# Storing a mixture-of-experts output before the last expert's rows are in, and adding those rows in memory by one accumulating transfer

## The chip, the cores and the metric

The kernel runs on one core of a Trainium2 chip. The metric is device time in microseconds (us) of one execution. The kernel before the change was timed three times: 296.11 us in the median, with 294.85 as the lowest and 299.49 as the highest.

## What is computed

One transformer block on an input `x` of 2 x 1024 tokens of 128 floats: a layer norm with a modulation, a gated DeltaNet attention with 16 heads of 8, a residual, a second layer norm, and then a mixture of experts. The last part is what the change is about:

```python
probs = softmax(h @ router_w.T)                     # 8 experts
k_probs, k_idx = top_k(probs, 2); k_probs /= sum    # two experts per token
# each expert takes its first `capacity` = 641 pairs (token, choice); later pairs give 0
h1 = silu(buf @ w1); out_buf = h1 @ w2              # per expert: 641x128 -> 512 -> 128
pair_out = out_buf[flat_e, slot] * keep
combined = sum over the token's two pairs of pair_out * k_probs
x = x + gb * (combined + h)
```

All is float32. There are 2048 tokens, 4096 pairs, and the output is 2048 x 128 floats, 1.05 MB.

## The kernel before, in words

Each engine has its own written program; the order of the work on an engine is the order of its code, and semaphores join the engines. The 2048 tokens are cut into four groups of 512 (`GROUPS = 4`), a group into four tiles of 128 tokens (`TG = 4`).

Attention, norms and routing run group by group up to about 192 us. In that time the rows that go to the experts are written by indirect transfers of GpSimd (POOL) into a table `dispatched` in memory. The residual with the gated normalised input stays in the on-chip tile `X`.

Then the eight experts follow, two buffers in turn (`u` is 0 or 1, `i` counts pairs of experts). For each one SyncE (SP) loads 640 rows and the weights, TensorE (PE) multiplies up (line 1876) and down (line 1893), ScalarE (ACT) applies silu (line 948), VectorE (DVE) scales the rows by the routing weight and the gate (line 1407), and POOL scatters them, 128 rows at a time, into the memory table `pair_out` (line 685). The 641st row of every expert is handled apart and scattered by line 698, seven experts' rows in a first transfer and the last expert's in a second.

`pair_out` has two parts, both cleared to zero early in the program. Rows 0 to 4095 hold one row per pair, for the first seven experts. Rows 4096 to 6143, 1.05 MB, are a table with one row per token, for the last expert alone; a token picks an expert at most once, so each token has at most one row there. The constant `to_token` turns a pair's row number into its token's row number for that.

The end of the program, after the scatters of the first seven experts have landed, goes so:

- SP loads the pair part in four transfers of 512 KB (line 599) into `yb`.
- DVE, per group, adds the two pairs of each token (`pair_sums`, line 1462) and the residual (`with_input`, line 1467) into `ys`. Between the first two of these it scales the very last 128 rows of the last expert.
- SP and ACT wait until the last expert's scatters have all landed (semaphores `rows_out1` and `last_rows_out`, lines 600, 601, 950 and 951), and then load the token part in four transfers of 256 KB into `yt` (line 603 by SP for groups 0 and 2, line 952 by ACT for groups 1 and 3).
- DVE adds `yt` to `ys` into `yo` (line 1478), group by group.
- SP and ACT store `yo` to the output (lines 606 and 955), 256 KB a group, and SP waits for the four stores (line 607).

Of the kernel before, what the change touches and what calls it, by code (L numbers as in the profile page):

```python
# [8 lines left out]
ALU = mybir.AluOpType  # L9
# [4 lines left out]
P = 128  # L14
B, S, DM = 2, 1024, 128
# [3 lines left out]
NE, FF = 8, 512  # L19
TOPK = 2  # L20
NTOK = B * S
PAIRS = NTOK * TOPK
# [6 lines left out]
TG = 4  # L29
GPB = S // (TG * P)  # L30
GROUPS = B * GPB
# [39 lines left out]
COL, _at = {}, 0  # L71
# [8 lines left out]
def constants():  # L80

    c = np.zeros((P, NCONST), np.float32)
    p = np.arange(P)
    r, t = p[:, None], p[None, :]
    same = r // BLK == t // BLK
    c[:, COL["ident"]] = np.eye(P)
    for i in range(NSUB):
        ref = (t // BLK) * BLK + i * SUB
        plus = same & (r >= ref) & (r <= t)
        minus = same & (r < ref) & (r > t)  # L90
        c[:, COL["gk"]][:, i * P:(i + 1) * P] = plus.astype(np.float32) - minus
        c[:, COL["kbias"]][:, i] = np.where(p % BLK < (i + 1) * SUB, 0.0, -1e4)
        c[:, COL["qbias"]][:, i] = np.where((p % BLK) // SUB == i, 0.0, -1e4)
    c[:, COL["own"]] = (r // SUB == t // SUB) & (r <= t)
    c[:, COL["cq"]] = same & (r <= t)
    c[:, COL["ck"]] = same & (r > t)
    c[:, COL["later"]] = np.where(r % BLK > t % BLK, -2.0 ** 100, 0.0)
    c[:, COL["hmask"]] = (p // DH % HG)[:, None] == np.arange(HG)[None, :]
    c[:, COL["smask"]] = (p // (C * DH))[:, None] == (np.arange(SW) // E1)[None, :]
    c[:, COL["tri"]] = r < t  # L100

    c[:, COL["spread"]] = r % (HALF * C) == t // DH
    col = np.arange(TG * 2 * BPT)[None, :] // BPT
    c[:, COL["tile_half"]] = (p // (HALF * C))[:, None] == col
    c[:, COL["blk"]] = (p // BLK)[:, None] == np.arange(BPT)[None, :]
    inv = (1.0 / 10000.0 ** (np.arange(0, DH, 2, dtype=np.float32) / np.float32(DH))).astype(np.float32)
    ang = (np.arange(S, dtype=np.float32)[:, None] * inv[None, :]).astype(np.float32)
    tab = lambda f: np.tile(f(ang).astype(np.float32).reshape(S // P, P, ROPE_HALF).transpose(1, 0, 2).reshape(P, -1), (1, B))
    c[:, COL["cos"]] = tab(np.cos)
    c[:, COL["sin"]] = tab(np.sin)  # L110

    c[:, COL["keep"]] = (np.arange(GROUPS) % GPB != 0)[None, :]
    c[:, COL["iota"]] = np.arange(NE)[None, :]
    g, at = np.divmod(np.arange(GROUPS * TG * TOPK), TG * TOPK)
    c[:, COL["pid"]] = (g * P + r) * TG * TOPK + at
    c[:, COL["to_token"]] = PAIRS + (g * P + r) * TG + at // TOPK - c[:, COL["pid"]]
    c[:, COL["batch_at"]] = np.where(p == NE - 1, PAIRS + NTOK // B, PAIRS // B)[:, None]
    c[:, COL["skip_last"]] = np.where((p == NE - 1)[:, None] == np.array([True, False])[None, :], 1e6, 0.0)
    return c
# [3 lines left out]
SYNC_OUT = list(range(0, GROUPS, 2))  # L123
SCALAR_OUT = list(range(1, GROUPS, 2))
# [30 lines left out]
def program(nc, x_d, wall_d, wo_d, rows_d, rwt_d, w1_d, w2_d, ct_d, wmod_d, const_d, bo_d, out_d):  # L155
    x_v = x_d.rearrange("b (g t p) c -> (b g) p t c", t=TG, p=P)
    out_v = out_d.rearrange("b (g t p) c -> (b g) p t c", t=TG, p=P)
    disp_d = nc.dram_tensor("dispatched", [ROWS, RW], F32, kind="Internal").ap()
    pair_d = nc.dram_tensor("pair_out", [PAIRS + NTOK, DM], F32, kind="Internal").ap()
    pair_v = pair_d[0:PAIRS, :].rearrange("(g p n) c -> g p (n c)", g=GROUPS, p=P)  # L160
    token_v = pair_d[PAIRS:PAIRS + NTOK, :].rearrange("(g p n) c -> g p (n c)", g=GROUPS, p=P)

    def w1_v(e):
        return w1_d[bass.ds(e, 1), :, :].rearrange("e p f -> p (e f)")
# [5 lines left out]
    with ctx:  # L170
# [3 lines left out]
        def sem(name):  # L174
            return ctx.enter_context(nc.semaphore(name))
# [3 lines left out]
        def event(name, per, ahead=None):  # L179
            e = Event(sem(name), per, ahead)  # L180
            if ahead:
                ahead_of[ahead].append(e)
            return e
# [36 lines left out]
        def carver():  # L220
            at = [0]

            def carve(*shape):
                n = int(np.prod(shape))
                v = arena[:, at[0]:at[0] + n]
                at[0] += n
                assert at[0] <= ARENA
                names = "abcd"[:len(shape)]
                return v.rearrange(f"p ({' '.join(names)}) -> p {' '.join(names)}", **dict(zip(names, shape)))

            return carve

        carve = carver()
# [69 lines left out]
        carve = carver()  # L303
# [12 lines left out]
        orow = carve(2, CT, DM)  # L316
        yb = carve(GROUPS, TG, TOPK, DM)
        ys = carve(GROUPS, TG, DM)
        yo = carve(GROUPS, TG, DM)
        yt = carve(GROUPS, TG, DM)  # L320
        row_gate = carve(CT, DM)
        gate_d = carve(DM)
        last_gate = carve(DM)
# [135 lines left out]
        osc = [event(f"rows_out{u}", 16 * CT) for u in range(2)]  # L459
        outs_left = [event(f"outs_left{u}", 1, "sp") for u in range(2)]  # L460
        s_lastO, s_lastR, s_lastS = sem("last_out_T"), sem("last_out_rows"), sem("last_rows_out")

        s_yb = [sem(f"pairs_in{g}") for g in range(GROUPS)]
        s_yt = [sem(f"tokens_in{g}") for g in range(GROUPS)]
        gates_done = event("row_gates", CT + 2)
        s_prep = sem("last_rows_prepared")

        s_ys, s_yo = sem("pairs_combined"), sem("out_ready")
        s_out = sem("out_written")

        def made(n, a):
# [31 lines left out]
        def rows_made(e, a):  # L503

            return a + 1 + (a > last_at(e))
# [7 lines left out]
        def apart(eng):  # L513


            eng.sem_inc(s_apart, 1)
# [7 lines left out]
        def _(sp):  # L524
# [72 lines left out]
            sp.wait_ge(osc[0].sem, osc[0].now(NE // 2 - 1) + 16)  # L597
            for g in range(GROUPS):
                sp.dma_start(yb[:, g].rearrange("p t k c -> p (t k c)"), pair_v[g]).then_inc(s_yb[g], 16)
            sp.wait_ge(osc[1].sem, osc[1].now(NE // 2 - 1))  # L600
            sp.wait_ge(s_lastS, 16)
            for g in SYNC_OUT:
                sp.dma_start(yt[:, g].rearrange("p t c -> p (t c)"), token_v[g]).then_inc(s_yt[g], 16)
            for g in SYNC_OUT:
                sp.wait_ge(s_yo, g + 1)
                sp.dma_start(out_v[g], yo[:, g]).then_inc(s_out, 16)
            sp.wait_ge(s_out, 16 * GROUPS)


        @block.gpsimd  # L610
        def _(pool):
# [68 lines left out]
            def rows_out(u, i, lo, hi):  # L680

                for a in range(lo, hi):
                    pool.wait_ge(r_done[u].sem, r_done[u].now(i, rows_made(2 * i + u, a)))
                    apart(pool)
                    pool.indirect_dma_start(pair_d, bass.IndirectOffsetOnAxis(ap=meta[:, u, a, 0:1].bitcast(U32), axis=0),  # L685
                                            orow[:, u, a, :], None, bounds_check=PAIRS + NTOK - 1, oob_is_err=False).then_inc(osc[u].sem, 16)
# [6 lines left out]
            def last_rows_out(n):  # L693

                pool.wait_ge(s_prep, 3)
                pool.wait_ge(s_lastR, n + 1)
                apart(pool)
                pool.indirect_dma_start(pair_d, bass.IndirectOffsetOnAxis(ap=last_idx[:, n:n + 1], axis=0),  # L698
                                        lastR[:, n, :], None, bounds_check=PAIRS + NTOK - 1, oob_is_err=False).then_inc(osc[0].sem if n == 0 else s_lastS, 16)
# [2 lines left out]
            rows_out(1, NE // 2 - 1, 0, FA)  # L702
            last_rows_out(1)
            rows_out(1, NE // 2 - 1, FA, CT)


        @block.scalar
        def _(act):
# [231 lines left out]
            for i in range(NE // 2):  # L940
                for u in range(2):
                    for k, (f, n) in enumerate(UPS):
# [3 lines left out]
                            act.wait_ge(r_ps[u].sem, r_ps[u].before(i))  # L946
                            act.wait_ge(last_done[u].sem, last_done[u].before(i))
                        a_.activation(hid[:, u, f, c0:c0 + cn], ps[:, k % 4, 0:cn], ACT.Silu).then_inc(hid_done[u].sem, 1)  # L948
            act.wait_ge(osc[1].sem, osc[1].now(NE // 2 - 1))
            act.wait_ge(s_lastS, 16)  # L950
            for g in SCALAR_OUT:
                act.dma_start(yt[:, g].rearrange("p t c -> p (t c)"), token_v[g]).then_inc(s_yt[g], 16)
            for g in SCALAR_OUT:
                act.wait_ge(s_yo, g + 1)
                act.dma_start(out_v[g], yo[:, g]).then_inc(s_out, 16)


        @block.vector
        def _(dve):
            v_ = nc.vector  # L960
# [4 lines left out]
            for u in range(2):  # L965
                f = v_.memset(v1[:, u, :, :, DH:E1], 1.0)
# [497 lines left out]
            def with_input(g):  # L1464

                dve.wait_ge(s_ys, 2 * g + 1)
                v_.tensor_tensor(ys[:, g].rearrange("p t c -> p (t c)"), ys[:, g].rearrange("p t c -> p (t c)"), X[:, g], ALU.add).then_inc(s_ys, 1)
# [4 lines left out]
            for g in range(1, GROUPS):  # L1472
                pair_sums(g)
                with_input(g)
            for g in range(GROUPS):
                dve.wait_ge(s_ys, 2 * g + 2)
                dve.wait_ge(s_yt[g], 16)
                v_.tensor_tensor(yo[:, g], ys[:, g], yt[:, g], ALU.add).then_inc(s_yo, 1)  # L1478


        @block.tensor
# [478 lines left out]
```

## Time and profile before

| what | us |
|---|---|
| median of three runs (lowest, highest) | 296.11 (294.85, 299.49) |
| the profiled execution | 293.68 |
| its span, first to last instruction | 291.9 |
| last matrix product ends | about 276.7 |
| last `ys` of the four groups ready | 281.98 |
| last scatter of the last expert landed | 281.95 |
| last `yo` ready | 287.88 |

The time of an execution is 1.8 us longer than its span. Over the span PE is busy for 86%, DVE for 72%, ACT for 42% and POOL for 31%; these are averages over stages, and in the last 15 us PE does nothing. An engine's name with a q (SPq, ACTq, POOLq) stands for its queue, where transfers are issued. A transfer has two times: that of its issue and the time to landing, counted from the start of the issue to the moment at which its semaphore is complete.

### The profile page before, as it was taken

What the parts mean: (1) busy time and instruction counts of PE and PEld (TensorE: products, weight loads), DVE (VectorE), ACT (ScalarE), POOL (GpSimd) and SP (SyncE); (2) the same over time, 40 slices, a digit from 0 to 9 for tenths busy, and PEclk for the clock granted to TensorE, in tenths of its full rate; (3) what the DMA queues carried; (4) which work ended last, traced back from release to release, by engine and by line L of the source; (5) the groups of instructions that cost most, each with busy time, mean ns of one, the idle gap of its engine ahead of it and who ended that gap; (6) DMA issues with size and microseconds to landing.
All of it is one profiled execution on the core that took longest, in us unless ns stands there. A gap on an engine that the chain in (4) does not pass through costs nothing. (4 is left out here: it accounts for less than half of the span.)

```text
span 291.9 us, 11345 instructions
## 1 busy us (share of the span) xinstructions
PE 251.4 (86%) x4731; PEld 188.4 (65%) x4731; DVE 209.2 (72%) x828; ACT 121.2 (42%) x274; POOL 90.0 (31%) x102
## 2 busy tenths in 40 slices
PE   7997898799977999899887889988999999999900
PEld 3665657676566855678555564436898889888800
DVE  5697989849699597986778568837557655756563
ACT  4598258652668444753322122203233432343200
POOL 0030014000023406052134216740544464546630
PEclk9999579779998799955999596999999999999965
DMA  6980000030700103000021001122424433331566
GB/s 178 338 311 4 3 2 6 4 146 4 291 4 4 30 3 112 13 4 12 22 80 46 21 6 57 45 80 86 129 55 130 147 96 108 121 100 36 172 214 227
DMA packets 18197, 25.19 MB, mean 86 GB/s; under 512 B 2679, under 2 KB 11400, under 8 KB 18146
## 3 DMA queue, kind: packets, MB, share of 16 engines
q1 hardware_dynamic: 14434, 19.18, 20.5%
q0 software_dynamic: 2368, 4.24, 4.5%
q10 hardware_dynamic: 1344, 1.05, 1.1%
q8 instruction: 37, 0.61, 0.9%
q14 instruction: 14, 0.11, 0.1%
HBM read 12.84 MB, written 12.15 MB: 86 GB/s over the span
## 5 line engine op out<-in xcount | busy, mean ns | idle before, releaser
L948 ACT ACTIVATE arena<-ps 128x385 f32<-128x385 f32 (+1 forms) x64 | 27.6, 439 | 62.3 <-PE ps L1876 61.6
L685 POOL DMA_INDIRECT pair_out<-arena,meta x40 | 39.2, 981 | 45.0 <-DVE arena L1407 19.2
L631 POOL DMA_INDIRECT dispatched<-row,idx x32 | 32.5, 1014 | 60.2 <-PE ps L1619 27.6
L1893 PE MATMUL ps<-w2t,arena 128*128 128x128 f32 x320 | 40.4, 278 | 0.0
L1893 PEld LDWEIGHTS ps<-w2t,arena 128*128 128x128 f32 x320 | 39.3, 191 | 0.9
L1512 PE MATMUL ps<-later_b,ident_b 128*128 128x512 bf16 x141 | 38.1, 409 | 0.0
L1876 PE MATMUL ps<-arena,w1t 128*128 128x256 f32 (+1 forms) x128 | 37.6, 434 | 0.2 <-issue 0.2
L1407 DVE SCALAR_TENSOR_TENSOR arena<-ps,meta,arena 128x128 f32<-128x128 f32 x40 | 14.0, 351 | 26.4 <-PE ps L1893 15.4
L654 POOL TENSOR_TENSOR arena<-arena,ex 128x256 f32<-128x256 f32 x16 | 10.7, 695 | 68.2 <-DVE arena L1029 50.2
L1612 PE MATMUL ps<-v,wts 32*32 32x9 f32 x2048 | 24.0, 180 | 8.8 <-issue 6.5
L1612 PEld LDWEIGHTS ps<-v,wts 32*32 32x32 f32 x2048 | 22.0, 117 | 13.5 <-issue 13.1
L1876 PEld LDWEIGHTS ps<-arena,w1t 128*128 128x128 f32 x128 | 22.9, 190 | 10.1 <-issue 0.9
L1507 PE MATMUL ps<-const,arena 128*128 128x128 f32 x120 | 21.1, 316 | 4.8 <-DVE arena L1029 3.0
L1512 PEld LDWEIGHTS ps<-later_b,ident_b 128*128 128x128 bf16 x141 | 13.6, 104 | 14.2 <-issue 3.9
L1507 PEld LDWEIGHTS ps<-const,arena 128*128 128x128 f32 x120 | 16.7, 165 | 8.1 <-DVE arena L1029 3.4
L1072 DVE SCALAR_TENSOR_TENSOR arena<-arena,dec,ps 128x18 f32<-128x18 f32 x128 | 19.7, 230 | 0.0
L827 ACT COPY s_sb<-ps 128x512 f32<-128x512 f32 x16 | 9.2, 577 | 23.0 <-PE ps L1654 23.0
L1541 PE MATMUL ps<-wall,hT 128*128 128x384 f32 x32 | 14.8, 590 | 0.7 <-ACT arena L753 0.5
L1654 PE MATMUL ps<-arena,fkT 32*32 32x128 f32 x512 | 13.2, 295 | 0.0
L978 DVE BATCH_NORM_STATS2 st<-ps 128x6 f32<-128x128 f32 x16 | 3.7, 287 | 13.2 <-PE ps L1694 13.2
L1009 DVE TENSOR_TENSOR arena<-arena,const 128x256 f32<-128x256 f32 x32 | 11.4, 420 | 2.1 <-ACT arena L753 2.0
L1094 DVE SCALAR_TENSOR_TENSOR wts<-s_sb,ps 128x512 f32<-128x512 f32 x16 | 10.9, 683 | 1.6 <-ACT s_sb L827 1.6
(182 smaller groups left out, 446.3 us busy)
## 6 DMA issues: line engine op xcount, KB each, us to landing
dispatched<-fill SPq DMA_DIRECT2D x12, 260.0 KB, 4.2
pair_out<-zero SPq DMA_DIRECT2D x6, 512.0 KB, 3.4
arena<-dispatched SPq DMA_DIRECT2D x8, 325.0 KB, 3.0
w1t<-in_w SPq DMA_DIRECT2D x8, 256.0 KB, 2.7
w2t<-in_w SPq DMA_DIRECT2D x8, 256.0 KB, 3.1
arena<-pair_out SPq DMA_DIRECT2D x4, 512.0 KB, 5.1
const<-in_constants SPq DMA_DIRECT2D x1, 803.5 KB, 6.5
X<-in_x SPq DMA_DIRECT2D x1, 768.0 KB, 7.6
```

Source lines behind the costliest of these rows:

```text
L631: pool.indirect_dma_start(disp_d, bass.IndirectOffsetOnAxis(ap=idx[:, p.g, t, k:k + 1], axis=0), row[:, p.g, t, k, :], None, bounds_check= ...
L685: pool.indirect_dma_start(pair_d, bass.IndirectOffsetOnAxis(ap=meta[:, u, a, 0:1].bitcast(U32), axis=0), orow[:, u, a, :], None, bounds_ch ...
L948: a_.activation(hid[:, u, f, c0:c0 + cn], ps[:, k % 4, 0:cn], ACT.Silu).then_inc(hid_done[u].sem, 1)
L1072: v_.scalar_tensor_tensor(state[:, (n + 1) % NB, a, :], state[:, n, a, :], dec[:, g % 2, at:at + 1], U_ps[:, a, j, :], ALU.mult, ALU.add). ...
L1407: v_.scalar_tensor_tensor(orow[:, u, a, :], row_bank(u, a)[:, 0:P], meta[:, u, a, 1:2], row_gate[:, a, :], ALU.mult, ALU.mult).then_inc(r_ ...
L1507: return nc.tensor.transpose(out, in_, ident[0:in_.shape[0], 0:in_.shape[0]])
L1512: mm(bank.rearrange("p (n c) -> p n c", c=P), ident_b[:], later_b[:].unsqueeze(1).to_broadcast([P, 4, P]), start=True, stop=True)
L1541: mm(proj_bank(g, t)[:, 0:3 * DM], hT[:, t * P:(t + 1) * P], wall[:, 0:3 * DM], start=True, stop=True).then_inc(proj.sem, 1)
L1612: mm(O_ps[r, h * E1:(h + 1) * E1], wts[r, t % 2, h, :], v1[r, g % 2, t, h, :], start=(h == 0), stop=False, skip_group_check=True, tile_pos ...
L1654: f = mm(ps[j * BLK:(j + 1) * BLK, hg, at:at + P], st(r), mv_(r), skip_group_check=True, tile_position=(hg * 32, j * BLK), **kw)
L1876: mm(ps[:, k % 4, 0:cn], w1t[:, u, f * P:(f + 1) * P], bT[:, u, c0:c0 + cn], start=True, stop=True).then_inc(up_ps[u].sem, 1)
L1893: m = mm(row_bank(u, a)[:, 0:P], hid[:, u, f, 1 + a * P:1 + (a + 1) * P], w2t[:, u, f, :], start=(f == 0), stop=(f == FT - 1))
```

## The change

The token part of `pair_out` is no longer loaded, and `yt` and `yo` are gone. SP and ACT store `ys`, the sum without the last expert's rows, as soon as DVE has it for a group. When the four stores and the last expert's scatters have all landed, POOL issues one transfer from memory to memory that adds the 1.05 MB token part to the output (`accum_op=ALU.add`). For this the token part is laid out in the order of the tokens, as the output is, which changes the constant `to_token`. SP waits for that transfer at the end.

```diff
-    c[:, COL["to_token"]] = PAIRS + (g * P + r) * TG + at // TOPK - c[:, COL["pid"]]
+    c[:, COL["to_token"]] = PAIRS + (g * TG + at // TOPK) * P + r - c[:, COL["pid"]]
...
-    token_v = pair_d[PAIRS:PAIRS + NTOK, :].rearrange("(g p n) c -> g p (n c)", g=GROUPS, p=P)
+    token_rows = pair_d[PAIRS:PAIRS + NTOK, :].rearrange("(r n) c -> r (n c)", r=P)
+    out_rows = out_d.rearrange("b s c -> (b s) c").rearrange("(r n) c -> r (n c)", r=P)
...
             for g in range(GROUPS):
                 sp.dma_start(yb[:, g].rearrange("p t k c -> p (t k c)"), pair_v[g]).then_inc(s_yb[g], 16)
-            sp.wait_ge(osc[1].sem, osc[1].now(NE // 2 - 1))
-            sp.wait_ge(s_lastS, 16)
             for g in SYNC_OUT:
-                sp.dma_start(yt[:, g].rearrange("p t c -> p (t c)"), token_v[g]).then_inc(s_yt[g], 16)
-            for g in SYNC_OUT:
-                sp.wait_ge(s_yo, g + 1)
-                sp.dma_start(out_v[g], yo[:, g]).then_inc(s_out, 16)
+                sp.wait_ge(s_ys, 2 * g + 2)
+                sp.dma_start(out_v[g], ys[:, g]).then_inc(s_out, 16)
             sp.wait_ge(s_out, 16 * GROUPS)
+            sp.wait_ge(s_added, 16)
...
             rows_out(1, NE // 2 - 1, FA, CT)
+            pool.wait_ge(osc[1].sem, osc[1].now(NE // 2 - 1))
+            pool.wait_ge(s_lastS, 16)
+            pool.wait_ge(s_out, 16 * GROUPS)
+            pool.dma_start(out_rows, token_rows, accum_op=ALU.add, max_dma_last_dim=4096).then_inc(s_added, 16)
...
-            act.wait_ge(osc[1].sem, osc[1].now(NE // 2 - 1))
-            act.wait_ge(s_lastS, 16)
             for g in SCALAR_OUT:
-                act.dma_start(yt[:, g].rearrange("p t c -> p (t c)"), token_v[g]).then_inc(s_yt[g], 16)
-            for g in SCALAR_OUT:
-                act.wait_ge(s_yo, g + 1)
-                act.dma_start(out_v[g], yo[:, g]).then_inc(s_out, 16)
+                act.wait_ge(s_ys, 2 * g + 2)
+                act.dma_start(out_v[g], ys[:, g]).then_inc(s_out, 16)
...
-            for g in range(GROUPS):
-                dve.wait_ge(s_ys, 2 * g + 2)
-                dve.wait_ge(s_yt[g], 16)
-                v_.tensor_tensor(yo[:, g], ys[:, g], yt[:, g], ALU.add).then_inc(s_yo, 1)
```

Nothing ahead of these places moves on any engine. The end of POOL's program (`rows_out1` is landings of the last scatters, `out_written` landings of the stores), before and then now:

```order
L698 DMA pair_out<-lastR,last_idx 6144x128 [waits last_rows_prepared,last_out_rows]
L685 DMA pair_out<-arena,meta 6144x128 [waits rows_done1] x2
L170 UNCONDITIONAL_BRANCH
```

```order
L694 DMA pair_out<-lastR,last_idx 6144x128 [waits last_rows_prepared,last_out_rows]
L681 DMA pair_out<-arena,meta 6144x128 [waits rows_done1] x2
L704 DMA out<-pair_out 256x1024 [waits out_written,last_rows_out,rows_out1]
L171 UNCONDITIONAL_BRANCH
```

POOL has one transfer more, of 256 pieces of 1024 floats (4 KB), behind all its scatters and behind the four stores. The end of ACT's program, before and then now (`pairs_combined` is the count of DVE's steps on `ys`, `out_ready` that of `yo`):

```order
L948 ACTIVATE arena<-ps 128x256 [waits up_ps1] x4
L952 DMA arena<-pair_out 128x512 [waits last_rows_out,rows_out1]
L952 DMA arena<-pair_out 128x512
L955 DMA out<-arena 128x4x128 [waits out_ready] x2
L170 UNCONDITIONAL_BRANCH
```

```order
L948 ACTIVATE arena<-ps 128x256 [waits up_ps1] x4
L951 DMA out<-arena 128x4x128 [waits pairs_combined] x2
L171 UNCONDITIONAL_BRANCH
```

ACT's two loads are gone, and its stores now wait for `ys`, no longer for `yo`; SP's end changes in the same way.

## Rows read from the trace of the kernel before

**Rows 1.** Chain of waits, its end: start us, us, what.

```profile
277.95 1.44 POOLq L170
279.39 0.30 issue
279.70 2.25 DMA pair_out<-arena,meta
281.95 0.02 issue
281.97 3.32 DMA arena<-pair_out
285.28 0.03 issue
285.31 0.02 DVEq L1477
285.33 0.04 issue
285.38 0.20 DVE arena L1478
...
286.92 0.09 issue
287.00 0.87 DVEq L170
```

**Rows 2.** Timeline, the last 12 us: start us, us, engine, line, op.

```profile
279.90 0.69 DVE L1467 TENSOR_TENSOR arena<-arena,X 128x512 f32<-128x512 f32 x1
280.56 0.69 DVE L1462 TENSOR_TENSOR arena<-arena 128x512 f32<-128x512 f32 x1
281.29 0.69 DVE L1467 TENSOR_TENSOR arena<-arena,X 128x512 f32<-128x512 f32 x1
...
285.38 2.50 DVE L1478 TENSOR_TENSOR arena<-arena 128x512 f32<-128x512 f32 x4 [3.40 <-DMA arena<-pair_out]
...
286.70 1.66 ACTq L955 DMA_DIRECT2D out<-arena  x2
```

**Rows 3.** ACT's stores, line 955: duration ns, starts, then time to landing.

```profile
L955 ACTq DMA_DIRECT2D out<-arena x2: 457/780/1102, 286.7 to 287.9; - x2
...
DMA to landing us min/median/max: 3.4/3.5/3.5
```

**Rows 4.** SP's stores, line 606, the same view.

```profile
L606 SPq DMA_DIRECT2D out<-arena x2: 388/388/389, 286.1 to 287.3; - x2
...
DMA to landing us min/median/max: 2.6/3.0/3.3
```

**Rows 5.** SP's four loads of the pair part, line 599, the same view.

```profile
L599 SPq DMA_DIRECT2D arena<-pair_out x4: 326/426/433, 272.7 to 274.0; - x4
...
DMA to landing us min/median/max: 3.6/5.1/6.5
```

**Rows 6.** ACT's two loads of the token part, line 952, the same view.

```profile
L952 ACTq DMA_DIRECT2D arena<-pair_out x2: 361/406/450, 282.0 to 282.4; - x2
...
DMA to landing us min/median/max: 3.6/4.0/4.5
```

**Rows 7.** Busy time of engines by stretch; last two columns: DMA share, GB/s.

```profile
273.70:280.10 6.40, 2.97 (x22) 2.56 (x20) 4.47 (x11) 1.16 (x3) 4.88 (x6) 0.97 0.97 352
283.20:286.00 2.80, 0.00 (x0) 0.00 (x0) 0.62 (x2) 0.00 (x0) 0.00 (x0) 0.50 0.97 360
287.00:291.00 4.00, 0.00 (x0) 0.00 (x0) 0.88 (x2) 0.00 (x0) 0.00 (x0) 0.50 0.85 262
...
280.00:281.00 1.00, 0.00 (x0) 0.00 (x0) 1.00 (x2) 0.00 (x0) 0.71 (x1) 0.50 0.10 26
281.00:282.00 1.00, 0.00 (x0) 0.00 (x0) 0.94 (x2) 0.00 (x0) 0.00 (x0) 0.50 0.14 41
```

**Rows 8.** Timeline, POOL's last three scatters (the first of eight rows).

```profile
276.57 1.24 POOL L698 DMA_INDIRECT pair_out<-lastR,last_idx  x1 [0.30 <-DVE arena L1407]
...
278.11 1.28 POOL L685 DMA_INDIRECT pair_out<-arena,meta  x1 [0.30 <-issue]
...
279.70 1.02 POOL L685 DMA_INDIRECT pair_out<-arena,meta  x1 [0.30 <-issue]
```

More of the change, by code:

```diff
@@ L318, in program @@
         ys = carve(GROUPS, TG, DM)
-        yo = carve(GROUPS, TG, DM)
-        yt = carve(GROUPS, TG, DM)
         row_gate = carve(CT, DM)
@@ L463, in program @@
         s_yb = [sem(f"pairs_in{g}") for g in range(GROUPS)]
-        s_yt = [sem(f"tokens_in{g}") for g in range(GROUPS)]
+        s_added = sem("last_expert_added")
         gates_done = event("row_gates", CT + 2)
         s_prep = sem("last_rows_prepared")
-        s_ys, s_yo = sem("pairs_combined"), sem("out_ready")
+        s_ys = sem("pairs_combined")
         s_out = sem("out_written")
```

## The prediction

> **What bounds the kernel now.** I read the chain of waits first, from its end backwards. It says that after the last matrix product only transfers and short adds are left [rows 1]: POOL's last scatter starts at 279.70 and has landed 2.25 us later, at 281.95; the load of the token part starts at 281.97 and the first group of it is there 3.32 us later; DVE adds, and the last part is the stores. The reader should see that 281.95 is a double point. DVE's last add of the residual starts at 281.29 and takes 0.69 us, so the last `ys` is ready at 281.98, 0.03 us after the scatter has landed [rows 1, 2]. Both branches of the tail, "sums without the last expert" and "rows of the last expert in memory", are ready at one time. All before that is the same in both kernels, so the prediction is about the 9.9 us from 281.98 to the span's end at 291.9.
>
> Those 9.9 us split so: token loads until DVE's first add at 285.38, which is 3.4 us; the four adds with their small gaps until 287.88, 2.5 us [rows 2]; ACT's last store, issued at 287.9 and landed 3.5 us later at 291.4 [rows 3]; and 0.5 us from there to the end. These are three steps in a row: read, add, write.
>
> The transfers are next, since the change trades one kind for another. A transfer here has a part that doesn't depend on its size. The four pair loads carry 4 x 512 KB = 2.10 MB: the first is issued at 272.7, the last at 274.0 and that one lands 6.5 us later, at 280.5; 7.8 us in all [rows 5]. The four token loads carry 1.05 MB: first issue 281.97 [rows 1], the last issue at 282.4, landed 4.5 us later at 286.9; 4.9 us in all [rows 6]. The difference is 2.9 us for 1.05 MB, so T = 2.0 us + 2.9 us for every 1.05 MB. The rates agree with that: 352 GB/s over the middle of the pair loads and 360 over that of the token loads, with the DMA engines 97% busy in both [rows 7]. Stores, which go in pieces of 512 bytes, run at 262 GB/s [rows 7]. POOL's last scatter, 64 KB, needs 2.25 us from its start to landing [rows 1], so a transfer issued by POOL has a fixed part of about 2.25 - 0.2 = 2.05 us, the same as above.
>
> **The change part by part.**
>
> *Taken away.* The four token loads and the wait for them (3.4 us), DVE's four adds (2.5 us). After 281.98 the old tail had load, add, store, end: 3.4 + 2.5 + 3.5 + 0.5 = 9.9 us, and only the last two kinds of term stay.
>
> *Stores of `ys`.* Groups 0, 1 and 2 are ready at about 278, 279.3 and 280.6 and their stores are out of the way early. The last isn't: its store can start only at 281.98. In the old tail the last stores took 3.3 and 3.5 us with two or three others in flight, and the first one, alone, 2.6 us [rows 3, 4]. Group 2's store, issued 1.4 us ahead, is still moving, so I take 3.3 us; ends 2.6 and 3.5.
>
> *What the early stores collide with.* From 277.9 to 280.5 the DMA engines are full of the pair loads [rows 7], and DVE has no slack: it begins the last pair sum at 280.56, just when the last load has landed (280.5) [rows 2, 5]. Group 0's store stands on SP's own queue behind the pair loads. Group 1's goes by ACT's queue, beside the last load. Its 0.26 MB is worth 0.26/0.36 = 0.7 us of transfer time if all of it went first, and less than half of the time does it overlap. I take 0.3 us on the last `ys`; ends 0 and 0.7. POOL's last scatter may be delayed too, which costs nothing: it is now needed only when the last store has landed, 3.6 us later.
>
> *The new wait.* POOL waits for scatters and stores; nothing is queued behind the transfer on POOL, and only SP's end waits for it. The scatters have long landed by then, so it is the store that holds it. From the release to the start of POOL's instruction I take 0.3 us, the gap that stands before each of its scatters [rows 8].
>
> *The accumulating transfer.* The trace of before has no such transfer, and none from memory to memory. Bounds from rows: it must at least move 1.05 MB, and if only that counts it costs what the token loads cost, 4.9 us. If all three passes (read the table, read the output, write it) count, at the rate of the stores, it is 2.05 + 3.15/0.262 = 14.1 us. Between them lies the case in which the two reads set the pace and the write runs beside them: 2.10 MB of reads in pieces of 4 KB is just what the pair loads are, 7.8 us. I take that, since in size, piece and direction of its reads that row is nearest; POOL's handling of 256 pieces in place of 128 I leave in it, because a scatter of 8 rows takes POOL 1.24 us and one of 128 rows 1.02 to 1.28 [rows 8]: it isn't the number of rows that costs.
>
> Here a page speaks for a smaller number. By the Trainium skill, "DMA: Bandwidth & Descriptors", section "Anatomy of one DMA — SWDGE (gpsimd) path", a transfer issued by GpSimd takes 2.0 us plus its bytes at 436 GB/s, 4.4 us for 1.05 MB, and the sum would be 3.4 us less than mine. The loads here ran at 352 and 360 GB/s, so the trace doesn't bear out the rate, though it does the 2.0 us. Another page speaks against the change: "Collectives: The Full Stack", section "The bandwidth ceiling: the fold count and why AG ≠ RS ≠ AR", says that a reducing transfer reads two sources through one read queue and so moves its result at half the rate of a copy, not that the add itself costs. No run here has shown that yet; it would put the transfer where the pair loads' row does.
>
> *The end.* 0.5 us from the last landing to the span's end, as before.
>
> *DVE, ACT, SP elsewhere.* The constant's change moves the last expert's rows in memory and leaves their number and size alone; nothing earlier in any engine's order changes. Costed at nothing; the cover for the scatters is the 3.6 us named above.
>
> **The sum.** 281.98 + 0.3 + 3.3 + 0.3 + 7.8 + 0.5 = 294.2 us of span, against 291.9: 2.3 us more. The old tail of 9.9 us becomes one of 12.2. The profiled execution took 293.68 us, so a like one would take 296.0. It lies 2.4 us under the median of the three runs (296.11), which scatter over 4.6 us. I set the difference on the median: 296.11 + 2.3 = 298.4 us.
>
> In short: two transfers follow each other in both tails. The change takes away an add of 2.5 us and starts the first of the two no earlier, and its second transfer carries two or three times the bytes of the store it replaces.
>
> **The rivals.** The price of the accumulating transfer decides, so the cases are cut by it. Each 2% is 5.9 us, which is also about what three runs that scatter by 4.6 us can tell from no change.
>
> *Forecast, 0.60.* The transfer takes 5.9 to 11.4 us, and the total is 296.5 to 302.0, most likely 298.4.
>
> *Rival 1, it is slow, 0.24.* Place: the memory-to-memory transfer. Mechanism: each piece needs its two reads and the write one behind the other, so that three passes are paid, not two. At 14.1 us it gives 298.4 + 6.3 = 304.7 us. It decides from 11.4 us on (7.8 + 5.9 - 2.3). For it: no row shows reads and writes of memory overlapped in one transfer, and the stores ran at 262 GB/s. Against it: the stores' pieces were 512 bytes and these are 4 KB.
>
> *Rival 2, the adding is nearly free, 0.14.* The second read hides and the transfer costs what a copy does, 4.9 us, and the last store, with nearly no company, lands in 2.6 us with no collision: 281.98 + 2.6 + 0.3 + 4.9 + 0.5 = 290.3, or 1.6 us less than before: 294.5 us. For it: the fixed part is the same for POOL. Against it: the DMA engines were at 97% with one read stream at 360 GB/s, so there's no room for a second. (The figure that the Trainium skill's "DMA: Bandwidth & Descriptors" gives, above, would come out on this side.)
>
> *Rival 3, the early stores take back time, within the above.* If all 0.79 MB of them stood before the last pair load and the last store, at 262 GB/s that is 3.0 us in place of the 0.3 I charged: 301.1 us. For it: the loads fill the engines until 280.5. Against it: from 280.5 to 281.98 the DMA engines are 10 to 14% busy, at 26 and 41 GB/s [rows 7], and the early stores can use that. I give it a tenth of the forecast's chance.
>
> *It doesn't do what it says, 0.02.* The stores would start early only for three groups out of four; that is in the sum. What is left is a gain that I don't see.
>
> Faster by over 2% would need a total of 290.2, under every case here: 0.02. Slower by over 2% is rival 1: 0.24. Within 2%: 0.74. The range has to hold 8 in 10: 295.3 leaves out the cheapest half of rival 2, and 304.5 the worst part of rival 1.
>
> **What would show it.** In the new profile: DVE's last add still ends at 282.0 to 282.6; the last store on ACT's queue starts right then and takes 2.6 to 3.5 us; POOL starts its transfer at 285.4 to 286.0, and its landing is 7.8 us later; in the DMA row the rate of bytes read from memory in that stretch is twice that of bytes written to it, near 350 GB/s for the reads. What would make the prediction wrong: a transfer that takes clearly more or less than 7.8 us from POOL's start; a DVE that waits for the last pair load by more than 0.7 us; or a POOL that needs several us before the first byte moves, which no row here shows.

## The result, and the profile after

The changed kernel takes 300.31 us in the median of four runs (299.07 to 303.9), the kernel before 295.48 us (its three runs of 296.11 in the median, and one more). The ratio is 1.0177, 95% interval [1.0108, 1.0247]: 3.2 to 7.3 us more, 5.2 us at the ratio itself. The interval takes in 2%, so whether the change costs more or less than 2% is not shown. Forecast were 2.3 us more. The total lies in the range and the sign is right; the size isn't, and the missing 2.9 us are the subject of what follows.

The ratios and intervals, here and below, leave out the slow runs, those over 1.5% above the kernel's fastest, and the profiled execution of the changed kernel is one of these (303.9 us). It is already 5 us late when the pair loads begin (277.7 us, against 272.7 before). Nothing in the code ahead of that place was changed, and in twelve profiles of ten kernels that stretch begins anywhere from 272.6 to 278.8 us. The two groups hardly overlap, though: it begins at 272.6 to 274.6 us in the four profiles of kernels with the old order of the token part, and at 274.4 to 278.8 in the eight with the new one, in whole or in part. Whether that is the change or chance is not shown. To compare what the change was meant to do, I measure the tail, from SP's first pair load to the end of the span. It was 291.9 - 272.7 = 19.2 us and 19.4 in the second profile of the kernel before; it is 302.1 - 277.7 = 24.4 us and 24.5 in the second profile of the changed one. The difference is 5.2 us, the same as that of the timed runs. A second timing of both doesn't narrow it: one execution of the changed kernel took 298.95 us and three took 305, and eleven of the kernel before took from 294.54 to 304.57.

The end of the chain of waits of the changed kernel (start us, us, what), which answers to [rows 1]:

```profile
286.72 0.70 DVE arena L1463
287.43 0.02 issue
287.45 2.48 DMA out<-arena
289.93 0.03 issue
289.95 0.04 POOLq L703
290.00 0.56 issue
290.56 1.04 POOLq L171
```

The last `ys` is ready at 287.43, ACT's last store lands 2.48 us later at 289.93, and POOL starts its transfer at 290.58. The chain stops there; what comes next has to be looked up by line. Line 704, POOL's accumulating transfer, and then line 171, where the closing instructions of all engines stand (engine, op, count: duration in ns, start):

```profile
L704 POOL DMA_DIRECT2D out<-pair_out x1: 1020/1020/1020, 290.6 to 290.6; - x1
...
DMA to landing us min/median/max: 8.1/8.1/8.1
```

```profile
L171 POOLq DRAIN  x1: 11284/11284/11284, 290.6 to 290.6; - x1
L171 SPq COMPARE_BRANCH  x1: 33/33/33, 298.8 to 298.8; - x1
L171 SPq DRAIN  x1: 74/74/74, 299.3 to 299.3; - x1
L171 SPq EVENT_SEMAPHORE  x1: 17/17/17, 302.0 to 302.0; - x1
L171 ACTq EVENT_SEMAPHORE  x1: 17/17/17, 302.0 to 302.0; - x1
```

The transfer lands at 298.7, 8.1 us after its start, and SP goes on at 298.8. But POOL's DRAIN, the closing instruction on its queue, runs from 290.56 for 11.28 us: until 301.84, which is 3.1 us after the landing. The last step of every engine, SP's and ACT's among them, starts only at 302.0, though ACT's own drain was over at 288.1: the engines meet at the end, and POOL is the last to come. In the list of waits of SP's queue the same 3 us look so:

```profile
SPq L603 <- DMA out<-pair_out: 12.5, 1, 12.5
...
SPq L171 <- PEq L171: 2.7, 1, 2.7
```

The second row names PE. PE had been done since 282, so the name is wrong; the row's use is that it says 2.7 us, where the kernel before has 0.2. Read the drains then.

The kernel before has this drain too, and its trace shows it:

```profile
L170 POOLq DRAIN  x1: 8888/8888/8888, 278.0 to 278.0; - x1
```

It ran from 277.95 to 286.84, 4.9 us past the landing of the last scatter at 281.95, and nobody waited for it, because loads, adds and stores went on until 291.4. In the second profile of the kernel before it ended 5.2 us ahead of the end of the span.

The accumulating transfer itself in the stretches view (last columns: DMA share and GB/s):

```profile
293.00:297.00 4.00, 0.00 (x0) 0.00 (x0) 0.00 (x0) 0.00 (x0) 0.00 (x0) 0.50 1.03 199
```

The DMA engines are as busy as in [rows 7], and the rate counted is only 199 GB/s. Behind the landing they have next to nothing to do: from 299 to 300 us their share is 0.02, and from 300 to 302 it is 0.00, while POOL's drain goes on.

### The profile page after: what moved, and what is told of

Same layout as the page of the kernel before. It is cut to its first block and busy times, and to the rows that moved or that the text cites. A ratio compares the mean times of both kernels' runs of the same rounds, so it can differ in the third digit from the quotient of the medians.

```text
span 302.1 us, 11334 instructions
## 1 busy us (share of the span) xinstructions
PE 253.1 (84%) x4731; PEld 189.3 (63%) x4731; DVE 206.6 (68%) x824; ACT 121.3 (40%) x274; POOL 92.0 (30%) x103
## 3 DMA queue, kind: packets, MB, share of 16 engines
HBM read 12.84 MB, written 13.20 MB: 86 GB/s over the span
## 5 line engine op out<-in xcount | busy, mean ns | idle before, releaser
L627 POOL DMA_INDIRECT dispatched<-row,idx x32 | 33.6, 1051 | 62.2 <-PE ps L1611 28.5
L1504 PE MATMUL ps<-later_b,ident_b 128*128 128x512 bf16 x141 | 35.6, 388 | 0.0
L1403 DVE SCALAR_TENSOR_TENSOR arena<-ps,meta,arena 128x128 f32<-128x128 f32 x40 | 14.0, 351 | 26.5 <-PE ps L1885 14.1
L1868 PEld LDWEIGHTS ps<-arena,w1t 128*128 128x128 f32 x128 | 22.9, 190 | 10.1 <-issue 0.9
L1604 PE MATMUL ps<-v,wts 32*32 32x9 f32 x2048 | 22.6, 177 | 6.5 <-issue 4.6
L1604 PEld LDWEIGHTS ps<-v,wts 32*32 32x32 f32 x2048 | 20.7, 111 | 10.8 <-issue 10.4
L1499 PE MATMUL ps<-const,arena 128*128 128x128 f32 x120 | 21.8, 321 | 6.0 <-DVE arena L1025 3.3
L974 DVE BATCH_NORM_STATS2 st<-ps 128x6 f32<-128x128 f32 x16 | 3.7, 285 | 14.2 <-PE ps L1686 9.9
```

What stands on the lines that cost most here:

```text
L627: pool.indirect_dma_start(disp_d, bass.IndirectOffsetOnAxis(ap=idx[:, p.g, t, k:k + 1], axis=0), row[:, p.g, t, k, :], None, bounds_check= ...
L1403: v_.scalar_tensor_tensor(orow[:, u, a, :], row_bank(u, a)[:, 0:P], meta[:, u, a, 1:2], row_gate[:, a, :], ALU.mult, ALU.mult).then_inc(r_ ...
L1499: return nc.tensor.transpose(out, in_, ident[0:in_.shape[0], 0:in_.shape[0]])
L1504: mm(bank.rearrange("p (n c) -> p n c", c=P), ident_b[:], later_b[:].unsqueeze(1).to_broadcast([P, 4, P]), start=True, stop=True)
L1604: mm(O_ps[r, h * E1:(h + 1) * E1], wts[r, t % 2, h, :], v1[r, g % 2, t, h, :], start=(h == 0), stop=False, skip_group_check=True, tile_pos ...
L1868: mm(ps[:, k % 4, 0:cn], w1t[:, u, f * P:(f + 1) * P], bT[:, u, c0:c0 + cn], start=True, stop=True).then_inc(up_ps[u].sem, 1)
```

## The experiments

All times "in the tail" count from the first pair load.

**POOL stores the last group, in the kernel before.** Is it this transfer, or any by POOL at the end, that leaves the drain exposed?

```diff
+            pool.wait_ge(s_yo, GROUPS)
+            pool.dma_start(out_v[GROUPS - 1], yo[:, GROUPS - 1]).then_inc(s_outp, 16)
...
-            for g in SCALAR_OUT:
+            for g in SCALAR_OUT[:-1]:
```

> The kernel before, with one edit: the store of the last group of the output is issued by POOL in place of ACT. In the changed kernel 3.1 us lie between the landing of POOL's transfer and the end of POOL's drain, the closing instruction of its program. Theory A (any transfer by POOL at the end leaves its drain exposed, whatever it carries): POOL's drain ends about 3 us after this store has landed, and the total is 2.5 to 4.5 us over the kernel before (3 us of drain, 0.6 us of slower issue by POOL). Theory B (only a long or accumulating transfer has that wait): the drain ends within 0.5 us of the landing and the total is 0 to 1.2 us over the kernel before.

Ratio to the kernel before 1.0189 [1.0082, 1.0296]; tail 23.0 us, 3.8 more. Its line 708 and POOL's drain:

```profile
L708 POOL DMA_DIRECT2D out<-arena x1: 810/810/810, 288.4 to 288.4; - x1
...
DMA to landing us min/median/max: 3.5/3.5/3.5
```

```profile
L170 POOLq DRAIN  x1: 7039/7039/7039, 288.3 to 288.3; - x1
```

The store starts at 288.38 and lands at 291.86, after the same 3.5 us as ACT's [rows 3]; it starts 0.5 us later in the tail than ACT's did. The drain ends at 288.35 + 7.04 = 295.39, 3.5 us after that. A plain store of 256 KB by POOL has the same wait behind it: theory A. In the old kernel, the choice of the engine that issues the last store is worth 3.8 us of tail.

**The copy without adding, by POOL.** The token part is copied over the output, which leaves all other sums out.

```diff
-            pool.dma_start(out_rows, token_rows, accum_op=ALU.add, max_dma_last_dim=4096).then_inc(s_added, 16)
+            pool.dma_start(out_rows, token_rows, max_dma_last_dim=4096).then_inc(s_added, 16)
```

> The changed kernel without the adding: POOL's last transfer copies the 1.05 MB token part over the output, which leaves the other sums out of the result. Theory A (the second read sets the accumulating transfer's pace): data moves at 350 GB/s or more, the transfer lands 4.9 to 5.5 us after POOL's start in place of 8.1, and the total is 2.6 to 3.2 us under the changed kernel. Theory B (memory to memory is slow by itself, or POOL's pieces are): 7.5 to 8.1 us, total the same. Either way POOL's drain ends about 3 us after the landing.

Ratio to the kernel before 1.0034 [0.9964, 1.0104]. Its transfer, and the DMA engines while it moves:

```profile
L704 POOL DMA_DIRECT2D out<-pair_out x1: 632/632/632, 287.2 to 287.2; - x1
...
DMA to landing us min/median/max: 5.2/5.2/5.2
```

```profile
289.00:291.50 2.50, 0.00 (x0) 0.00 (x0) 0.00 (x0) 0.00 (x0) 0.00 (x0) 0.50 0.91 365
```

5.2 us in place of 8.1, tail 21.4 in place of 24.4, and the drain ends 3.1 us after the landing again. The copy moves at 365 GB/s and the adding transfer at 199, with busy engines in both. So adding costs 2.9 us here, and that much of theory A is shown; its reason, a second read, is not. The page's count of bytes is the same for the changed kernel and for the copy:

```profile
HBM read 12.84 MB, written 13.20 MB: 86 GB/s over the span
```

This is the line of the changed kernel. The kernel before has 12.84 MB read too, and 12.15 written. So no second read of 1.05 MB is counted: either this count leaves it out, or the 2.9 us are some other cost of adding that grows with the bytes. The first fits the price, since a second read of 1.05 MB costs 2.9 us by [rows 5, 6]. The Trainium skill, "Collectives: The Full Stack", section "The bandwidth ceiling: the fold count and why AG ≠ RS ≠ AR", says of collective operations that a reduction moves at half the rate of a copy because it reads two sources. The trace agrees with the rate, at 0.55 of the copy's, and can't show the reason.

**The copy without adding, by SP.**

```diff
             sp.wait_ge(s_out, 16 * GROUPS)
+            sp.dma_start(out_rows, token_rows, max_dma_last_dim=4096).then_inc(s_added, 16)
             sp.wait_ge(s_added, 16)
```

> The same copy without adding, issued by SP in place of POOL, after the same waits. Theory A (POOL's part costs its drain, 3 us, and about 0.5 us of issue): against the copy by POOL the total is 3 to 4 us less, and the span ends 0.3 to 0.7 us after the landing. Theory B (the 3 us stand behind any memory-to-memory transfer): the same 3 us after the landing here, total 0 to 1 us under the copy by POOL.

Only the profile is telling: the medians are 297.77 us and 297.87 for the kernel before, without an interval. The transfer:

```profile
L605 SPq DMA_DIRECT2D out<-pair_out x1: 618/618/618, 289.0 to 289.0; - x1
...
DMA to landing us min/median/max: 5.4/5.4/5.4
```

```profile
L171 POOLq DRAIN  x1: 8868/8868/8868, 282.4 to 282.4; - x1
L171 SPq COMPARE_BRANCH  x1: 38/38/38, 294.4 to 294.4; - x1
...
L171 SPq EVENT_SEMAPHORE  x1: 17/17/17, 294.7 to 294.7; - x1
```

It lands as the other copy does, 5.4 us after its start, and the span ends 0.4 us later: POOL's drain, now behind its last scatter again, was over at 291.24. The tail is 17.8 us, 3.6 less than with the same copy by POOL. So the 3 us belong to the issuing engine and not to transfers from memory to memory: theory A. The timed runs don't show these 3.6 us: the medians of the two copies, 298.57 us by POOL and 297.77 by SP, are 0.8 us apart, with runs that scatter by over 6.

**Adding by group.** Four accumulating transfers, each behind its own group's store.

```diff
-            pool.wait_ge(s_out, 16 * GROUPS)
-            pool.dma_start(out_rows, token_rows, accum_op=ALU.add, max_dma_last_dim=4096).then_inc(s_added, 16)
+            for g in range(GROUPS):
+                pool.wait_ge(s_outg[g], 16)
+                pool.dma_start(out_rows[g], token_rows[g], accum_op=ALU.add, max_dma_last_dim=4096).then_inc(s_added[g], 16)
```

> The changed kernel with its one accumulating transfer cut into four, one per group, each waiting only for its own group's store. Theory A (the time goes into a serial chain of last store, then 1.05 MB accumulated, then drain): only the last 0.26 MB stand behind the last store; the last transfer lands 3.5 to 4.5 us after its start in place of 8.1, total 3.5 to 4.5 us under the changed kernel, 0.5 to 1.5 us over the kernel before. Theory B (the accumulating transfers run one after the other with a cost each, 2 us or more of it fixed): the last one queues behind the three ahead of it and lands 6 us or more after its start, total within 2 us of the changed kernel.

Ratio to the kernel before 1.0226 [1.0061, 1.0391]; tail 22.7 us. Line 706:

```profile
L706 POOL DMA_DIRECT2D out<-pair_out x4: 917/1234/1417, 286.7 to 288.8; - x4
...
DMA to landing us min/median/max: 4.4/5.9/7.0
```

The last one needs 7.0 us for a quarter of the bytes, since it stands behind the others; from the first start to the last landing it is 9.0 us (286.7 to 295.8). Cutting wins 1.7 us of tail against the one transfer, not 3.5 to 4.5: theory B. The first of the four starts 2.7 us earlier in the tail than the one transfer, but all four together take 0.9 us longer. The timed runs don't show a gain (1.0226 against 1.0177, with wide intervals). The drain ends 3.2 us after the last landing.

**Pieces of 8 KB** in the accumulating transfer (`max_dma_last_dim=8192`).

> The changed kernel with pieces of 8 KB in place of 4 KB in the accumulating transfer, 128 in place of 256. Theory A (bytes read set its pace): 8.1 us again, within 0.3 us. Theory B (a cost for each piece, in POOL or in the DMA engines): 1 us or more less.

```profile
L704 POOL DMA_DIRECT2D out<-pair_out x1: 956/956/956, 288.7 to 288.7; - x1
...
DMA to landing us min/median/max: 7.8/7.8/7.8
```

Half as many pieces and 0.3 us at most: the number of pieces isn't the price. That is what theory A expected, but it only rules out a cost for each piece; it doesn't show what the bytes wait for. One execution of this kernel was timed (301.71 us).

**Stores held back** until all four sums are ready.

```diff
-                sp.wait_ge(s_ys, 2 * g + 2)
+                sp.wait_ge(s_ys, 2 * GROUPS)
```

(and the same on ACT)

> The changed kernel, but no group's sums are stored before all four are ready. Theory A (the early stores delay the last pair load, and with it the last sum, by about 0.4 us, and win 1.5 to 2.5 us by being out of the way): last sum ready 9.3 us after the first pair load's issue in place of 9.7, but the last store lands 4.0 to 5.0 us after that in place of 2.5; the span's end comes 1.2 to 2.2 us later than in the changed kernel, 25.6 to 26.6 us after the first pair load. Theory B (early stores win nothing, since the stores are limited elsewhere): the end within 0.5 us of the changed kernel's.

The last sum is ready at 9.4 us in the tail, the last store landed at 14.9, 5.5 us later, and the tail is 27.1 us, 2.7 more than the changed kernel's. So the early stores are worth 2.7 us, more than the 1.2 to 2.2 I had expected. This is one profile; its execution, the only one timed, took 307.01 us. What they cost can't be told: the last `ys` is ready at 9.7 and 10.1 us in the two profiles of the changed kernel and at 9.3 with pieces of 8 KB, but at 9.3 and 9.7 in the two of the kernel before, which has no early stores.

**The changed kernel and the kernel before, once more.**

> The changed kernel once more, unedited, for a second profile. If the split read from its first profile holds, then from the first pair load's issue to the span's end it takes 24.4 us again (19.2 in the kernel before): accumulating transfer 8.1 us, and 3.1 us from its landing to the end of POOL's drain. If the first profile was a disturbed one, the stretch is shorter by 1 us or more.

> The kernel before once more, unedited, for a second profile. The stretch from the first pair load's issue to the span's end repeats within 0.2 us of 19.2, and POOL's drain ends 4 to 5 us after its last scatter has landed, about 4.8 us before the end of the span, so that nobody waits for it. What differs from profile to profile is the time at which that stretch begins.

Changed: tail 24.5 us, transfer 7.9, drain's end 3.1 us after its landing. Before: tail 19.4 us, drain's end 14.2 in the tail, 5.2 before the end. The splits hold.

**Half added, half the old way.** Groups 0 and 1 stored early and then added in memory by one transfer of 0.52 MB, groups 2 and 3 as before.

```diff
+    own = np.where(g < ADDED, (g * TG + at // TOPK) * P + r, (g * P + r) * TG + at // TOPK)
...
+            pool.wait_ge(s_early, 16 * ADDED)
+            pool.dma_start(out_rows, token_rows, accum_op=ALU.add, max_dma_last_dim=4096).then_inc(s_added, 16)
...
-            for g in range(GROUPS):
+            for g in range(ADDED, GROUPS):
                 dve.wait_ge(s_ys, 2 * g + 2)
                 dve.wait_ge(s_yt[g], 16)
```

> A mixture: groups 0 and 1 are stored early and get the last expert's rows by one accumulating transfer of 0.52 MB; groups 2 and 3 go the old way, load, add, store. If it is POOL's drain and the serial chain that cost the change its time, both branches run beside each other here: POOL's transfer starts about 10.3 us after the first pair load's issue, lands 5 to 6 us later, its drain ends 3.2 us after that, at 18.5 to 19.5 us; the old branch ends at 17.5 to 18.5. Total against the kernel before: 0 to 0.7 us less. If the two branches slow each other in the DMA engines by more than their overlap wins: 0.5 to 2 us more than before.

```profile
L176 POOLq DRAIN  x1: 8727/8727/8727, 286.7 to 286.7; - x1
...
L176 SPq COMPARE_BRANCH  x1: 37/37/37, 294.0 to 294.0; - x1
```

The tail is 19.2 us, no shorter than before. SP has both branches at 294.0, and POOL's drain ends at 286.65 + 8.73 = 295.38: without it the tail would be near 18, by estimate (294.0 - 276.4 and the 0.4 us of the end). The two branches do run beside each other; the drain takes the win back. The timed runs say more, though: a ratio of 1.019 [1.0113, 1.0268]. The tail doesn't show these 1.9%, so they lie ahead of it: the profiled execution begins its tail at 276.4 us, against 272.7 and 274.6 in the two of the kernel before. Ahead of the tail this kernel's instructions are those of the kernel before; only the rows of the token part are in another order, as in the changed kernel. Why it starts late is open, and with it whether the new order costs time there.

**The old tail in eight pieces**, each half a group, nothing by POOL.

```diff
-                sp.dma_start(out_v[g], yo[:, g]).then_inc(s_out, 16)
+            q.dma_start(out_v[g][:, t0:t0 + 2], yo[:, g, t0:t0 + 2]).then_inc(s_out, 16)
```

(loads and adds cut in the same way)

> The kernel before with its last three steps (load the token part, add, store) cut into eight pieces of half a group in place of four of one group; no POOL transfer at the end. If the old tail is a chain in which the stores, at 262 GB/s, begin only when the first load of 256 KB has landed and been added, a first piece half as large lands 0.5 to 0.8 us earlier and the add is 0.35 us shorter: from the first pair load's issue to the span's end 17.9 to 18.6 us in place of 19.2, a total 0.2 to 0.4% less than before, which the timed runs can hardly show. If the cost of issuing twice as many transfers (0.4 us each on SP and ACT) stands on the path instead, 19.2 us or more.

Ratio 0.9973 [0.9943, 1.0003]; tail 19.0 us. A miss, between the two: the first store starts 0.8 us earlier than before (12.6 against 13.4 in the tail), but the last one 0.9 us later (16.1 against 15.2). The last load is issued 1.7 us after the first, in place of 0.4, and lands 1.3 us later in the tail (15.5 against 14.2); DVE waits 1.0 us for the fifth half, and a half's add takes 0.42 us, not 0.35. How much of that is the issuing of more transfers, and how much the first stores moving beside the last loads, isn't told apart. Faster by 0.3% if at all, and not shown beyond the noise.

## Why the prediction was right in sign and short in size

The steps of the sum, with the times of the changed kernel's first profile (second one in brackets):

| step | forecast | measured |
|---|---|---|
| last `ys` ready, later than before | 0.3 | 0.4 (0.8) |
| last store to landing | 3.3 | 2.5 (2.5) |
| release to POOL's start | 0.3 | 0.65 (0.65) |
| accumulating transfer | 7.8 | 8.1 (7.9) |
| last landing to the end of the span | 0.5 | 3.3 (3.3) |
| tail against before | +2.3 | +5.2 (+5.3) |

- **The double point** held: what the change takes away and what it adds both begin at the last `ys`.
- **The accumulating transfer** is right in size: 7.8 forecast, 8.1 and 7.9 measured. The choice of the pair loads [rows 5] as the nearest row is borne out in its price: the copy costs 5.2 us, nearly the lower bound of 4.9, and adding costs what a second read of 1.05 MB would. That it is a second read stays argued. The sign that I had named for it, a rate of reads near 350 GB/s and twice that of writes, wasn't seen: the view gives 199 GB/s, and the bytes counted are those of a copy. Rival 1 (14.1 us) and rival 2 (4.9 us) are out by the time measured.
- **The last store** was charged 0.8 us too much: the early stores leave the DMA engines nearly to it alone, and it takes what the first store took in [rows 4]. The collision that I charged 0.3 us for isn't seen apart from the spread between profiles. Rival 3 is out: holding the stores back costs 2.7 us.
- **The gap at POOL** is 0.65 us, not 0.3: the 0.3 us of [rows 8] are the time behind POOL's own instruction before, while here 0.56 us of "issue" stand behind the end of the queue's wait, in both profiles of the changed kernel.
- **The end** is the step that failed. "0.5 us from the last landing to the span's end, as before", and with it "nothing is queued behind the transfer on POOL, and only SP's end waits for it". POOL's own drain stands behind it and ends 3.1 us after the landing. I had read 0.5 us off a program whose last transfer is ACT's and used it for one whose last transfer is POOL's. Of the missing 2.9 us it is all but 0.1; the other four errors are +0.1, -0.8, +0.35 and +0.3, and that they cancel is luck. That the total lies in the range is owed to the range's width, too: made for the price of the transfer, it reached from 0.8 us less to 8.4 us more than before. The store by POOL in the old kernel, +3.8 us, and the copy by SP, -3.6 us, show it from both sides.

The row that would have told was in the trace of before: a POOLq DRAIN of 8888 ns that ended 4.9 us after the last scatter's landing. In the page's chain it stood as "POOLq L170" [rows 1], on the way between two scatters, and I took it for part of them. The prediction named the cover of POOL's scatters; it should have named that of POOL's end.

With 3.3 us in place of 0.5 for the end, the forecast would have been 294.2 + 2.8 = 297.0 us of span, 5.1 us more than before, against 5.2 measured.

## What to carry to other kernels

Before a kernel's last transfer goes to another engine, read from the trace what each engine does after its last landing: the closing drain of the engine that issues it becomes part of the time, and while it is covered it costs nothing and no list of waits shows it. Price a transfer by the passes over memory that it makes, from a row that makes as many; an add "for free" on the way cost 2.9 us for 1.05 MB, as much as a second read would. And if runs scatter by more than the change is worth, measure from an anchor ahead of the changed part: the tail repeats within 0.1 and 0.2 us while the start of it wanders by 6.

## What was not expected of the hardware

POOL's drain ends 3.1 to 3.5 us after the landing of POOL's last transfer in all eight profiles in which that transfer stood at the end of the program: 3.1 and 3.1 in the changed kernel, 3.1 with pieces of 8 KB, 3.1 with the stores held back, 3.1 for a copy, 3.2 for four transfers, 3.1 for half the bytes, 3.5 for a plain store. It is 3.1 us with adding and without, and for 0.52 MB as for 1.05 MB. Behind the last scatter, in the kernel before, it was 4.9 us. What it does in that time the traces don't show. ACT's and SP's drains take 0.16 us and less, and don't wait so for a store in flight: ACT's is over at 288.6 in the kernel before, 2.9 us before its last store lands.
